# Score spreading by two transfers instead of TensorE, and a rearranged batch loop, in a cross-attention and routed feed-forward kernel

## The reference, cut to what matters

```python
x = x + xattn(layernorm(x), ctx, ctx, mask, w_q, w_k, w_v, w_o)   # 16 heads of 16, 8 batches, 512 queries, 1024 keys
x = x + ffn(layernorm(x), w_router, W_qkv, W_out, g1, g2, W1, W2, W3)
# ffn: scores = x @ w_router
#      _, idx = top_k(scores, 128)            # 128 of a batch's 512 rows, in order of their scores
#      h = rmsnorm(x[idx], g1); causal self-attention of the 128 rows; gated feed-forward of 682; rows put back at idx
```

## Time and profile before

| | |
|---|---|
| median of 3 runs | 877.21 us (876.47 to 877.97) |
| the profiled execution | 877.64 us, of which its span is 875.8 us |
| TensorE matmul busy | 844.8 us, 96% of the span |
| ScalarE busy | 563.7 us, 64% |
| VectorE busy | 327.6 us, 37% |
| GpSimd busy | 123.3 us, 14% |
| mean granted TensorE clock | 0.998 |

### The profile page before, as it was taken

The page is one execution under the profiler, slowest core; times in us unless marked ns, Lnnn a source line. Parts: engine busy times, 40 slices in busy tenths (PEclk is TensorE's granted clock), DMA queues, the critical chain, the costliest instruction groups (busy, mean ns, idle before and its releaser), DMA issues. The chain is left out here.

```text
span 875.8 us, 27999 instructions
## 1 busy us (share of the span) xinstructions
PE 844.8 (96%) x11618; PEld 288.9 (33%) x11618; DVE 327.6 (37%) x945; ACT 563.7 (64%) x634; POOL 123.3 (14%) x174
## 2 busy tenths in 40 slices
PE   7999999999999999999999999999999999999875
PEld 2322222324323332334323333234323342234333
DVE  3132254323443345423543234522454223322452
ACT  3577657676677767677577766677666766877310
POOL 3100112021020111101111110201111111200111
PEclk9999999999999999999999999999999999999999
DMA  6080230111301220201301202012202100010000
GB/s 187 5 292 4 67 85 9 56 41 41 80 14 51 80 69 16 58 26 57 80 15 49 79 18 65 14 51 80 55 5 59 32 2 7 16 48 3 8 25 11
DMA packets 37706, 42.91 MB, mean 49 GB/s; under 512 B 3251, under 2 KB 32478, under 8 KB 37576
## 3 DMA queue, kind: packets, MB, share of 16 engines
q1 hardware_dynamic: 35080, 39.08, 15.1%
q0 software_dynamic: 2496, 1.98, 1.2%
HBM read 31.20 MB, written 12.60 MB: 50 GB/s over the span
## 5 line engine op out<-in xcount | busy, mean ns | idle before, releaser
L561 ACT ACTIVATE probs<-pair_bank 128x1024 f32<-128x1024 f32 x512 | 496.3, 1021 | 228.4 <-ACTq L560 226.4
L531 PE MATMUL pair_bank<-q_sb,k_sb 32*64 32x512 f32 x4096 | 293.9, 612 | 0.9 <-PEq L529 0.9
L550 PE MATMUL o_bank<-probs,va 128*32 128x512 f32 x2048 | 273.2, 604 | 2.7 <-PEq L547 1.2
L531 PEld LDWEIGHTS pair_bank<-q_sb,k_sb 32*64 32x64 f32 x4096 | 64.6, 129 | 145.3 <-issue 143.1
L550 PEld LDWEIGHTS o_bank<-probs,va 128*32 128x32 f32 x2048 | 41.7, 108 | 206.8 <-issue 114.6
L304 PE MATMUL m_bank<-wv_sb,ctx_in 128*32 128x256 f32 x1024 | 62.5, 380 | 2.7 <-PEq L319 2.7
L304 PE MATMUL m_bank<-ctx_in,wk_sb 128*32 128x512 f32 x480 | 61.0, 592 | 0.0
L701 DVE TENSOR_SCALAR va<-m_bank,valid 128x256 f32<-128x256 f32 x64 | 28.1, 479 | 81.9 <-DVEq L698 81.6
L642 DVE STREAM_TRANSPOSE o_blk<-o_bank 128x512 f32<-128x512 f32 x32 | 22.9, 717 | 76.7 <-DVEq L641 76.7
L304 PEld LDWEIGHTS m_bank<-wv_sb,ctx_in 128*32 128x32 f32 x1024 | 33.8, 110 | 39.5 <-issue 25.5
L1000 POOL DMA_INDIRECT in_order<-y_tok,place x28 | 29.2, 1042 | 101.9 <-POOLq L999 84.3
(11 more groups left out here) (177 smaller groups left out, 593.7 us busy)
## 6 DMA issues: line engine op xcount, KB each, us to landing
ctx_in<-in_ctxT SPq DMA_DIRECT2D x7, 1024.0 KB, 5.0
x<-in_x SPq DMA_DIRECT2D x8, 512.0 KB, 4.7
mask_in<-in_mask SPq DMA_DIRECT2D x8, 512.0 KB, 3.9
out_dram<-base SPq DMA_DIRECT2D x8, 512.0 KB, 5.4
x_in<-in_x SPq DMA_DIRECT2D x28, 128.0 KB, 4.2
turned<-blocks_t SPq DMA_DIRECT2D x28, 128.0 KB, 3.2
xn_t<-turned SPq DMA_DIRECT2D x7, 512.0 KB, 3.9
ctx_in<-in_ctxT SPq DMA_DIRECT2D x2, 512.0 KB, 7.6
```

The costliest lines, as they stand in the source:

```text
L531: last = nc.tensor.matmul(pair_bank[pairs[r // 2]][j:j + 64, r % 2], key_tile(b, s, r)[:, j:j + 64], query_tile(b, s, r), start=True, stop ...
L550: last = nc.tensor.matmul(o_bank[32 * r:32 * r + 32], va[b % 2][:, t, HV * h:HV * h + 32], probs[s % 2][:, r], start=(t == 0), stop=(t == ...
L561: nc.scalar.activation(probs[s % 2][:, 2 * e:2 * e + 2, :], pair_bank[p][:], ACT.Exp, scale=HD ** -0.5).then_inc(s_free[p], 1)
```

## The change

The transposes and the copy of `spread` leave the loop for b > 0 (after the loop, for the last batch, they stay). In their place SyncE stores `score` to DRAM, waits for that, and loads it back to every partition as `scores_in`; VectorE reorders this into `all_scores` ahead of `order0`. In the loop V1 moves from step 11 to steps 6 and 7 in halves, K01 from 18 and 19 to 8 and 9, R0 from 9 and 10 to 10 and 11, V3 from 21 to 18 and 19 in halves, K10 from 23 to 21, and the `differ` of ScalarE from 21 to 23. VectorE's V1 now stands between `order0` and `order1`, and its V3 ahead of `pv`.

```diff
-           ("P", "K11:0", 4, False), ("P", "K11:1", 5, False), ("F", "spread", 6, False),
-           ("P", "R0:0", 9, False), ("P", "R0:1", 10, False), ("P", "V1", 11, False), ("P", "R1:0", 12, False), ("P", "R1:1", 13, False),
+           ("P", "K11:0", 4, False), ("P", "K11:1", 5, False), ("P", "V1:0", 6, False), ("P", "V1:1", 7, False), ("P", "K01:0", 8, False),
+           ("P", "K01:1", 9, False), ("P", "R0:0", 10, False), ("P", "R0:1", 11, False), ("P", "R1:0", 12, False), ("P", "R1:1", 13, False),
            ("F", "hidT", 14, False), ("F", "q", 15, False), ("F", "k", 16, False), ("F", "v", FS_STEP, False),
-           ("F", "fs", FS_STEP, False), ("P", "V2", FS_STEP, False), ("P", "K01:0", 18, False), ("P", "K01:1", 19, False),
-           ("F", "pv", 20, False), ("P", "V3", 21, False), ("F", "wout", 22, False), ("P", "K10", 23, False), ("F", "hid2T", 24, False),
+           ("F", "fs", FS_STEP, False), ("P", "V2", FS_STEP, False), ("P", "V3:0", 18, False), ("P", "V3:1", 19, False),
+           ("F", "pv", 20, False), ("P", "K10", 21, False), ("F", "wout", 22, False), ("F", "hid2T", 24, False),
...
-ACT_SLOT = [("P", "K00", 0), ("P", "K11", 5), ("F", "spread", 6), ("F", "hidT", 14),
-            ("F", "v", FS_STEP), ("F", "fs", FS_STEP), ("P", "K01", 19), ("P", "differ", 21), ("P", "K10", 23), ("F", "hid2T", 24),
+ACT_SLOT = [("P", "K00", 0), ("P", "K11", 5), ("P", "K01", 9), ("F", "hidT", 14),
+            ("F", "v", FS_STEP), ("F", "fs", FS_STEP), ("P", "K10", 21), ("P", "differ", 23), ("F", "hid2T", 24),
...
-             ("F", "order1"), ("N", "norm0"), ("F", "order2"), ("F", "order3"), ("P", "R0"), ("P", "V1"), ("F", "selected"), ("P", "R1"),
-             ("F", "base"), ("F", "q"), ("N", "norm1a"), ("F", "k"), ("N", "norm1b"), ("P", "V2"), ("F", "pv"), ("P", "V3"), ("F", "wout"),
+             ("P", "V1"), ("F", "order1"), ("N", "norm0"), ("F", "order2"), ("F", "order3"), ("P", "R0"), ("F", "selected"), ("P", "R1"),
+             ("F", "base"), ("F", "q"), ("N", "norm1a"), ("F", "k"), ("N", "norm1b"), ("P", "V2"), ("P", "V3"), ("F", "pv"), ("F", "wout"),
...
+        def spread_scores(sp):
+            sp.wait_ge(score_ready, 1)
+            sp.sem_inc(score_ready, -1)
+            sp.dma_start(score_row.rearrange("(p t) -> p t", t=QT), score[:]).then_inc(score_stored, 16)
+            sp.wait_ge(score_stored, 16)
+            sp.sem_inc(score_stored, -16)
+            sp.dma_start(scores_in[:], score_row.partition_broadcast(P)).then_inc(spread_in, 16)
...
-                if t == 0 and i == MISC:
+                if t == 0 and note is put:
+                    dve.wait_ge(spread_in, 16)
+                    dve.sem_inc(spread_in, -16)
+                    nc.vector.tensor_copy(all_scores[:].rearrange("p (t q) -> p t q", t=QT),
+                                          scores_in[:].rearrange("p (q t) -> p t q", t=QT))
+                    dve.drain()
+                elif t == 0 and i == MISC:
...
                     if b > 0:
+                        spread_scores(sp)
                         load_selected(sp, b - 1)
```

More of the change, by code:

```diff
@@ L179, in program @@
         in_order = nc.dram_tensor("in_order", [CAP, D + 1], F32, kind="Internal").ap()
+        score_row = nc.dram_tensor("score_row", [S], F32, kind="Internal").ap()
+        scores_in = sb("scores_in", [P, S])
         x_res = sb("x_res", [P, D])
@@ L227, in program @@
         rows_read, rows_copied = sem("rows_read"), sem("rows_copied")
+        score_stored, spread_in = sem("score_stored"), sem("spread_in")
         place_ready, rows_placed, xtok_in = sem("place_ready"), sem("rows_placed"), sem("xtok_in")
```

## The result

The changed kernel takes 882.61 us as a median (881.72 to 883.75), against 877.29 for the kernel before in the same comparison: a ratio of 1.0063, 95% interval 1.005 to 1.0076. It is slower by 5.3 us. The forecast was 875.4, with a range to 881.0. The profiled execution took 881.72, its span is 880.0, and the mean granted clock is 0.992.

What follows compares the result with a forecast made beforehand. TensorE's queue and its holes were taken to bound the kernel. Step 11 -3.8, other steps 0.0 and batch 7 +2.0 gave -1.8: 875.8 for the profiled execution, 875.4 as a median, range 871.0 to 881.0.

Steps and rivals of the forecast that it cites:

- The steps of a batch: TensorE's step lengths in a batch: 23.80 us before and after, `differ` included, so the change wins nothing there (0.0).
- (b): Step 25: slack of the third pair of banks takes up `differ`; 872.5, or 871.0 with all of it free; chance 0.18.
- (e): The hole in step 11 has another cause and moves to where R1 wants the bank; 879.2; chance 0.10.
- (d): V1's read-out is held behind the first indirect DMA: 1.0 in each of six batches, 881.4; partly held 877 to 880; chance 0.18.
- Step 11: V1 waits there for R0's read-out, late behind GpSimd's fourth indirect DMA; the hole goes, -3.8 over five batches.
- The transfers: Score store 2.5, broadcast load 2.65, waits and issues 0.5: together 5.7 us, bounds 4.5 and 7.6; cost only in batch 7.
- (c): Transfers take 7.6; steps 8 and 9 stand 0.6 in six batches, batch 7 1.9 longer; 880.9; chance 0.12.
- Batch 7: The last batch: scores come late, TensorE stands 2.6 in step 9; net +2.0, with bounds +0.8 to +3.9.
- Then `differ`: ScalarE's mask check, moved into empty step 23, delays the exponentials: 0.74 in step 25 per batch, bounds 0.25 and 1.33.

## Why the prediction was wrong

**The steps of a batch: right.** 2.90 for steps 6 to 9 and 11, 2.04 for 23, 2.75 for 24 (2.76 foretold), all six batches. The exponentials' model for `differ` gave 0.74; 0.75 was measured. The rivals that wanted other lengths fell with this: (b), for step 25 is longer; (e), for step 12 is 2.90; (d), for steps 8 and 9 are 2.90.

**Step 11: right where the hold is.** -3.8 was foretold and came; the experiment that holds the DMA back shows the cause that the prediction read from a distance of 1.5. The hold is in the profile that the prediction was read from and in profiles from two chips of the comparisons; on a third chip the term is 0, and there the -3.8 would have been missed.

**The transfers: right in sum, wrong in parts.** 5.7 from ready scores to landed ones, as forecast, so (c) fell too. The store takes 1.4 and not 2.5, the broadcast 3.7 and not 2.65: the two errors cancel, which is luck. The Trainium skill (DMA: Bandwidth & Descriptors, Anatomy of one DMA) has a rule for a DMA that GpSimd issues: 2.0 us or so fixed, and the bytes at 436 GB/s. SyncE's two transfers don't follow it: the store's 1.4 lies below the fixed part alone, and the broadcast's 3.7 above the 2.6 that the rule would make of 256 KB (an estimate).

**Batch 7: +2.0 foretold, +1.7 measured,** with a stop of 2.74 where 2.6 was worked out. The sum hides an error: the low clock behind the stop, 1.2, wasn't in it, nor were 1.8 that later steps gave back.

**The step that failed** is "Then `differ`". The prediction put its cost at 0.74 a batch, "all of it" at most 1.33, and had no term for what it releases. It priced ScalarE's 1.3 us and stopped there. `differ` also frees the mask's buffer, SyncE's load waits for that, and the context's load waits behind it. The prediction counted SyncE's queue for the transfers of `spread_scores`, but not for the stage that it moved. Two loads that had left 7 us apart leave as one burst of 7 us; a block of TensorE's instructions stands behind it; and TensorE, which runs 96% full, stops, which makes the step 2.6 longer (5.91 where the clock stayed up), and runs 3.4 at half its clock, another 1.7. That is 4.2 of the 5.9 by which the profiled execution missed the forecast (881.72 less 875.8), shown from both sides: putting the context first closes the hole, and moving `differ` alone opens it in the kernel before. Batch 1's step 17 adds 1.3, by another late block that the prediction didn't have either. The tail's 0.9 can't be put down to the change: it is 61.8 long here and 60.1 in the changed kernel's second profile, and the low clock in it is in the second profile of the kernel before as well. None of the rivals had an engine that waits for its own instructions, so the range ended 1.6 too low.

By the Trainium skill (SBUF — State Buffer, Who interferes with whom) a DMA never contends with a compute engine. That speaks of ports, and no run here speaks against it there; but a block of instructions is a DMA too, and by its late coming the loads did stop TensorE.

What stays open: why the hold after an indirect DMA is there on some chips and not on one; why the clock falls behind some stops and not behind others; and whether the fetch waits for the burst in a ring or for the memory.

## What to carry to other kernels

When a stage is moved, follow the buffer that it frees to the DMA queue: which load is released, what stands behind it, and which bursts then join. A wait put down to "issue" on an engine that is 96% busy was, each time it was longer than 0.25 here, a missing block of instructions; look in the DMA view for the queue of kind "instruction" and for loads that run ahead of it, and break the burst by the order of the loads before anything else. A gain that rests on a hole of unknown cause should be priced down, since the hole may be absent on the next chip.

## What the runs showed of the hardware

- A block of 16 KB of TensorE's instructions stood behind a burst of 1.7 MB of loads: the block that came at 199.1 in the kernel before came at 203.3, at the burst's end, and TensorE was idle for 1.4 by the profile (3.3 in another execution).
- Behind the hole of the first profile (2.2 without work), and behind batch 7's stop of 2.74 on a semaphore, TensorE ran at the lower level of its clock (1.2 GHz) for 3.4 us; 48 products behind the hole took 2.54 instead of 1.49, and the low clock cost 1.7 there. It isn't so behind every stop: of all stops within the loop of 1.38 to 3.27, on "issue" or on a semaphore, nine had the low clock right behind them, and nine, one of 3.01 among them, had not.
- A read-out by VectorE that was due 0.63 behind an indirect DMA of GpSimd started 1.52 behind it, and with the DMA issued later it wasn't late; step 11 was as long in profiles from two chips of the comparisons, and on a third the same code starts 0.63 behind the DMA, with nothing lost.
- In the changed kernel the transfer of a block of some 250 instructions began 1.2, as a median, behind TensorE's start on the block before it; behind the end of a late one TensorE took 1.2 to 1.5 to go on.
